# First feed-forward of a macaron layer: batches 4 to 7 go through a list of rows sorted by expert, in 15 tiles of 512 rows, instead of through all eight experts

## The chip, the core and the metric

The kernel runs on one core of a Trainium2 chip, in float32. The metric is the device time of one execution in microseconds (us). TensorE (PE) multiplies, VectorE (DVE), ScalarE (ACT) and GpSimd (POOL) work on its results, SyncE (SP) issues most of the DMAs. Each engine runs its own list of instructions strictly in the order in which they are written, and waits for the others by semaphores.

## The reference, cut to what matters

x is (8, 512, 128): 8 batches of 512 tokens. The layer is x + 0.5 FFN(norm(x)), then attention with 16 heads, then x + 0.5 FFN(norm(x)) again. The feed-forward:

```
probs = softmax(einsum('bsd,de->bse', x, gate_w) + gate_b, axis=1)     # over the tokens of a batch
vals, idx = top_k(probs, 2)                                            # 2 of 8 experts for each token
h = relu(einsum('bsd,edo->ebso', x, w1) + b1)                          # w1, w2, w3: (8, 128, 128)
h = relu(einsum('ebso,eop->ebsp', h, w2) + b2)
y = relu(einsum('ebso,eop->ebsp', h, w3) + b3)
w_tok = einsum('bske,bsk->bse', one_hot(idx), vals)                    # 0 for the experts not chosen
v = einsum('ebso,bse->eo', y, w_tok)                                   # one row for each expert, over all tokens
out = einsum('bse,eo->bso', one_hot(idx).max(axis=2), v)
```

A token's y for an expert counts only by its weight in v, and that weight is 0 for six of the eight experts. v sums over all tokens of all batches, so nothing behind it starts before the last of them is done.

## The kernel before, in words

**Units.** A feed-forward f (0 or 1) is 32 units (NU, line 43): unit u takes batches 2p and 2p+1 (p = u // 8), 1024 tokens as two halves of 512 columns, through expert e = u % 8. Each float32 product is three TensorE passes (high weights x high data, low x high, high x low), so a unit is 3 layers x 3 passes x 2 halves = 18 matmuls of 512 columns (`product` L739, `layer2` L758). DVE does the first activation in two instructions of 1024 columns (`split1_high` L1475, `split1_low` L1481). ACT does the second in two halves, relu and rounding (`relu2`, L1144 to L1167); POOL subtracts to get the low part (`split2`, L682). DVE does the third together with the weighting by w_tok and the sum over tokens in one instruction with an accumulator (`reduce3`, L1564 to L1577). The weights for that, spread to all 128 partitions, are in PU; one DMA of 512 KB for each unit, issued by SP, brings them from the DRAM tensor wd (`load_wb`, L509).

**Order.** `unit_steps` (L410) is one list that all engines walk: in iteration u stand layer 1 of unit u+2, its split, layer 2 of unit u+1, layer 3 of unit u, and then extra steps of a table (`GATE1` for the first feed-forward, L396). The PSUM pairs are a ring of four (`ring_table`, L234): each use waits until the use four earlier was drained.

**The gate of batches 4 to 7** is spread over iterations 0 to 12 by GATE1: normalize (ACT), transpose (PE), copy twice (ACT), low part (POOL), logits (PE), softmax, four steps of top-2 (`choose_late`, L1627), and the weights. The gate of batches 0 to 3 and the splitting of the weights are in `head` (DVE's from L1521), ahead of the units. Behind the units `update(0)` (L1685) turns the sums into the rows added to x; attention starts on them.

## Time and profile before

| | us |
|---|---|
| median of 3 runs | 1057.64 |
| lowest and highest of them | 1049.88, 1057.66 |
| profiled execution: span from the first to the last instruction | 1048.3 |
| device time given for the profiled execution itself | none; the lowest run is 1.6 above its span |
| busy share of the span: PE, DVE, ACT, POOL | 97%, 73%, 60%, 67% |
| granted TensorE clock, mean | 0.997 of full |

The first feed-forward's units run from about 18 to 176 us of the span, attention to about 900 us, the second feed-forward to the end. Shares of busy time are means over these stages. PE is called busy while a matmul is in flight, so 97% does not say that it could do no more; a stretch in which its matmuls start at a fixed distance does.

### The profile page before, as it was taken

Reading aid. Unit: us, or ns where it says so; the run is one execution under the profiler, and the core shown is the slowest. Engines: PE = TensorE matmul, PEld = TensorE weight load, DVE = VectorE, ACT = ScalarE, POOL = GpSimd, SP = SyncE. Lnnn points to the kernel's source line nnn. Section 1 sums busy time; section 2 is a strip of 40 time slices with the busy share of each in tenths; the row PEclk is TensorE's granted clock in tenths of the full one; section 3 lists DMA queues with packets and bytes.
Section 4 is the critical chain, followed back from the end, with each engine's and each line's share of the span. In section 5 each row is a group of like instructions: output and inputs, shape, how many; then the busy total and the mean of one; then the engine's idle time right before and its main releaser. Section 6 shows DMA issues by size and latency. Waiting matters only on the chain.

```text
span 1048.3 us, 18768 instructions
## 1 busy us (share of the span) xinstructions
PE 1015.9 (97%) x7176; PEld 661.9 (63%) x7176; DVE 763.9 (73%) x1027; ACT 632.1 (60%) x900; POOL 700.0 (67%) x369
## 2 busy tenths in 40 slices
PE   7999998899999999999999999999999999998996
PEld 6676886545657566556655665745565565776884
DVE  6879998877875676567576587546757636779996
ACT  4785556756754565456475477467746456775553
POOL 5555655766886588488488578756849757565653
PEclk9999999999999999999999999999999999999999
DMA  5721520000100100001001010001000103521612
GB/s 169 237 86 58 183 84 21 1 2 23 42 23 22 42 24 22 22 23 43 22 23 43 3 42 23 22 25 40 22 23 23 42 25 102 182 81 49 209 67 81
DMA packets 30253, 59.62 MB, mean 57 GB/s; under 512 B 10437, under 2 KB 15702, under 8 KB 30166
## 3 DMA queue, kind: packets, MB, share of 16 engines
q1 hardware_dynamic: 30096, 58.41, 18.4%
q8 instruction: 58, 0.95, 0.4%
q14 instruction: 29, 0.24, 0.1%
q10 hardware_dynamic: 70, 0.02, 0.0%
HBM read 55.27 MB, written 2.62 MB: 55 GB/s over the span
## 4 chain that ended last, share of the span: by engine, by line
PE 83%; DVE 10%; ACT 2%; issue 2%; POOL 2%; DMA 0%; DVEq 0%; ACTq 0%; POOLq 0%
PE ring L1038 20%; PE ring L972 6%; PE ring L1050 6%; PE ring L996 5%; PE ring L1002 5%; PE ring L998 5%; PE ring L1000 5%; PE ring L742 4%; PE ring L748 4%; PE ring L744 4%; PE ring L1011 3%; PE ring L766 2%; PE ring L765 2%; PE ring L768 2%; DVE ring L1576 2%
## 5 line engine op out<-in xcount | busy, mean ns | idle before, releaser
L1728 DVE TENSOR_REDUCE mx<-ring 128x2 f32<-128x1024 f32 x248 | 290.3, 1226 | 64.1 <-PE ring L972 64.1
L627 POOL TENSOR_TENSOR sum_picksT<-sum_picksT,P_wb 128x1024 f32<-128x1024 f32 x128 | 310.7, 2427 | 18.9 <-POOL sum_picksT L627 0.9
L1356 ACT ACTIVATE P_wb<-ring 128x1024 f32<-128x1024 f32 x256 | 262.1, 1026 | 54.2 <-PE ring L1002 24.6
L627 POOL TENSOR_TENSOR sum_picksT<-P_wb 128x1024 f32<-128x1024 f32 x64 | 167.0, 2610 | 167.8 <-ACT P_wb L1356 167.8
L686 POOL TENSOR_TENSOR R<-t,R 128x512 fp32r<-128x512 f32 x124 | 162.1, 1308 | 124.5 <-ACT R L1166 121.2
L1038 PE MATMUL ring<-P_wb,t 128*32 128x512 f32 x2048 | 228.4, 593 | 0.0
L1038 PEld LDWEIGHTS ring<-P_wb,t 128*32 128x32 f32 x2048 | 74.0, 110 | 138.6 <-issue 120.0
L1368 ACT COPY OZ<-ring 128x512 f32<-128x512 f32 x64 | 37.4, 585 | 157.3 <-PE ring L1038 148.6
L1166 ACT CAST R<-t 128x512 fp32r<-128x512 f32 x124 | 76.9, 620 | 74.6 <-PE ring L748 68.2
L972 PE MATMUL ring<-R 64*128 64x512 f32 x512 | 104.8, 407 | 1.0 <-ACT P_wb L1344 0.7
L996 PE MATMUL ring<-R 64*128 64x512 f32 x512 | 102.0, 393 | 1.5 <-DVE MR L1733 1.5
L1000 PE MATMUL ring<-R 64*128 64x512 f32 x512 | 101.1, 390 | 0.0
L998 PE MATMUL ring<-R 64*128 64x512 f32 x512 | 101.0, 390 | 0.0
L1002 PE MATMUL ring<-MR,NEG 64*128 64x512 f32 x496 | 98.3, 392 | 0.0
L1162 ACT ACTIVATE t<-ring,bcol 128x512 f32<-128x512 f32 x124 | 84.8, 684 | 20.8 <-PE ring L768 20.3
L1576 DVE SCALAR_TENSOR_TENSOR ring<-ring,nb,P_wb 128x1024 f32<-128x1024 f32 x62 | 80.0, 1290 | 13.3 <-PE ring L748 13.2
L742 PE MATMUL ring<-R,whi 128*128 128x512 f32 x252 | 81.5, 404 | 6.1 <-DVE MR L1485 1.8
L748 PE MATMUL ring<-R,whi 128*128 128x512 f32 x252 | 79.6, 396 | 0.0
L744 PE MATMUL ring<-R,wlo 128*128 128x512 f32 x252 | 79.6, 396 | 0.0
L972 PEld LDWEIGHTS ring<-R 64*128 64x128 f32 x512 | 48.2, 184 | 36.9 <-issue 24.9
L1753 DVE TENSOR_TENSOR OT_xnT<-OZ,rzb 128x1024 f32<-128x1024 f32 x32 | 70.0, 2188 | 0.0
L996 PEld LDWEIGHTS ring<-R 64*128 64x128 f32 x512 | 47.9, 184 | 34.6 <-ACT P_wb L1356 29.7
(199 smaller groups left out, 1529.9 us busy)
## 6 DMA issues: line engine op xcount, KB each, us to landing
P_wb<-wd SPq DMA_DIRECT2D x64, 512.0 KB, 4.8
rzb<-rzd SPq DMA_DIRECT2D x64, 256.0 KB, 3.9
xs<-in_L_attn_x SPq DMA_DIRECT2D x8, 256.0 KB, 5.2
zrc<-SZ SPq DMA_DIRECT2D x128, 2.0 KB, 1.7
out<-xs SPq DMA_DIRECT2D x8, 256.0 KB, 2.7
sum_picksT<-in_L_ffn_w SPq DMA_DIRECT2D x2, 512.0 KB, 5.6
MR<-mT SPq DMA_DIRECT2D x62, 4.0 KB
t<-in_L_ffn_w SPq DMA_DIRECT2D x1, 512.0 KB, 7.3
```

The source lines that it names most:

```text
L627: pool.tensor_tensor(US[:, g % 2, c, :, :], first, PU[:, TPB * c + t, :, :], ALU.add).then_inc(s_ua, 1)
L686: pool.tensor_tensor(low[:, k, :], t2[:, k, :], high[:, k, :].bitcast(F32), ALU.subtract).then_inc(s["h2_ready"], 1)
L742: pe.matmul(pair[:, k, :], whi[:, layer, e, :], high[:, k, :], start=True, stop=False)
L744: pe.matmul(pair[:, k, :], wlo[:, layer, e, :], high[:, k, :], start=False, stop=False)
L972: mm = pe.matmul(banks[:, par, :], QH[g % len(QH)][rows, c, P * j:P * (j + 1)], KH[rows, g // QUADS % 2, :], start=True, stop=True)
L996: pe.matmul(banks[:, par, :], KH[rows, kv, keys], QH[g % len(QH)][rows, c, :], start=True, stop=False)
L998: pe.matmul(banks[:, par, :], KH[rows, kv, keys], QL[g % len(QL)][rows, c, :], start=False, stop=False)
L1000: pe.matmul(banks[:, par, :], KL[rows, kv, keys], QH[g % len(QH)][rows, c, :], start=False, stop=False)
L1002: mm = pe.matmul(banks[:, par, :], less[rows, :], MR[rows, g % 2, c, :], start=False, stop=True)
L1038: mm = pe.matmul(weigh_bank(g, c)[row:row + SLOT, :], Vn[:, g // QUADS % 2, t, d:d + SLOT], PU[:, TPB * c + t, par, :], start=(t == 0), st ...
L1356: act.activation(PU[:, u, :, :], ring[slot(("scores", g, u))][:, :, :], ACT.Exp, scale=SCALE).then_inc(s_exp, 1)
L1728: dve.tensor_reduce(mx[:, :, u] if g else mx0_unit[:, u // TPB, :, 0, u % TPB, 0], ring[slot(("max", g, u))][:, :, :], AX.X, ALU.max).then ...
```

## The change

Only the first feed-forward changes in what it runs; units 0 to 15 (batches 0 to 3) stay. For batches 4 to 7 the 2048 tokens x 2 choices = 4096 rows are put into a DRAM list `rows_by_expert`, sorted by expert; each expert's part begins at a multiple of 512 rows (a tile). A row is 128 normalized values and 8 weights, 544 bytes. 15 tiles (8 + 7 for parts that are not full) run always; rows that nobody fills are zeros, written by 5 DMAs at the start. So units 16 to 31 become 8 units of two tiles (the last of one), 7.5 in place of 16.

- **Head:** POOL clears 1632 columns of `MR`, SP writes them five times to the list (4.2 MB). `MR` is also the buffer of unit 1's first activation: DVE waits for the five writes before `split1(0, 1)`.
- **Iterations 1 to 8:** normalized values go to `rows`; the copies to xh and xl for batches 4 to 7 go away; logits of four batches are taken at once; the four steps of top-2 stand in iterations 6 and 7 instead of 8 to 12. In 8, `count_rows` and `place_rows` work out each row's place and `tile_tables` each tile's expert and biases.
- **Iterations 8 to 12:** POOL sends the rows: 32 indirect DMAs of 128 rows, 7 in each iteration (4 in the last), behind its split2. In these iterations the second half of split2 is DVE's.
- **End of 12:** POOL copies the 768 columns of weights of tiles 0 to 7 to a buffer indexed by tile, two more tiles in each of iterations 16 to 19.
- **From 13 on:** each iteration begins with a `gather` for unit u+3: SP has loaded the rows, PE turns them (4 transposes for each tile), ACT rounds, DVE gets the row weights and the low part. SP writes the weights of a unit's rows out and spreads them back to PU.

```diff
+        RT = GROUPS * TPB * TPB * P // TS + E - 1
+        UNITS_OF = (DENSE + RU, NU)
+        def low_by_dve(f, u, k):
+            if f:
+                return k == 1 and u >= NU - 2
+            return u == UNITS_OF[0] - 1 or (k == 1 and SCATTERS.start <= u < SCATTERS.stop)
+        SCATTERS = range(8, 13)
-                 1: [("invert", 2), ("normal", 4)],
-                 2: [("turn", 4), ("normal", 5)],
-                 3: [("turn", 5), ("logits", 4), ("normal", 6)],
-                 4: [("turn", 6), ("logits", 5), ("normal", 7)],
-                 5: [("turn", 7), ("logits", 6)],
-                 6: [("logits", 7), ("largest", 1), ("exp", 1)],
-                 7: [("invert_sum", 1), ("probs", 1)],
-                 8: [("turn_probs", 1), ("choose", 0)],
-                 9: [("choose", 1)],
-                 10: [("choose", 2)],
-                 11: [("choose", 3)],
-                 12: [("picks", 1)]}
+                 1: [("invert", 2), ("normal", 4), ("normal", 5)],
+                 2: [("turns", 4), ("normal", 6), ("normal", 7)],
+                 3: [("turns", 6)],
+                 4: [("logits4", 4)],
+                 5: [("invert_sum", 1), ("probs", 1)],
+                 6: [("turn_probs", 1), ("choose", 0), ("choose", 1)],
+                 7: [("choose", 2), ("choose", 3)],
+                 8: [("counts", 1), ("ranks", 1)]}
+        for u in range(SCATTERS.start, SCATTERS.stop):
+            n = u - SCATTERS.start
+            GATE1.setdefault(u, []).extend(("scatter", k) for k in range(7 * n, min(7 * n + 7, 2 * TPB * TPB)))
+        GATE1[SCATTERS.stop - 1] += [("copy", r) for r in range(4)]
+        for r in range(4, RU):
+            GATE1.setdefault(DENSE + r - 4, []).append(("copy", r))
...
+            for u in range(last):
+                if u + 3 < last and routed(f, u + 3):
+                    steps.append(("gather", u + 3))
...
+            for part in range(5):
+                sp.dma_start(xg.rearrange("(p q r) c -> q p (r c)", p=P, q=5)[part], zeros).then_inc(s_zf, 16)
...
+                sp.wait_ge(s_sent, 16 * 2 * TPB * TPB)
+                routed_weights()
...
+            def scatter(n):
+                if n == 0:
+                    pool.wait_ge(s_places, 3)
+                    pool.wait_ge(s_zf, 16 * 5)
+                t = n % (TPB * TPB)
+                pool.indirect_dma_start(out=xg[:, :], out_offset=bass.IndirectOffsetOnAxis(ap=row_of[:, n:n + 1], axis=0),
+                                        in_=rows[:, t, :], in_offset=None).then_inc(s_sent, 16)
+            def copy_weights(r):
...
+                for k in halves_of(0, DENSE + r):
+                    e = pool.value_load(expert_int[0:1, 2 * r + k:2 * r + k + 1], min_val=0, max_val=E - 1)
+                    ins = pool.tensor_copy(WT[:, r % 4, k, :, :, :].rearrange("p l h o -> p (l h o)"),
+                                           wex[:, bass.ds(e, 1), :, :, :].rearrange("p e l h o -> p (e l h o)"))
...
+            def sorted_low(u):
+                r, n = u - DENSE, len(halves_of(0, u))
+                k = r % 2
+                dve.wait_ge(s_sorted[k], 16 * (r // 2 + 1))
+                wait(dve, s_rwd, 16 * (r - 1))
+                tiles = of_expert[:, 2 * r:2 * r + n, :].unsqueeze(2).to_broadcast([P, n, BLOCKS, E])
+                choice_link(dve.tensor_tensor(row_products[k][:, 0:n, :, :], sorted_rows[k][:, 0:n, :, P:ROW], tiles, ALU.mult))
+                dve.tensor_reduce(row_weights[k][:, 0:n, :], row_products[k][:, 0:n, :, :], AX.X, ALU.add).then_inc(s_rw, 1)
+                high, low = x_of(0, u)
+                dve.wait_ge(s_rxh, r + 1)
+                dve.tensor_tensor(low[:, 0:n, :], unit_pair(0, "gather", u)[:, 0:n, :], high[:, 0:n, :].bitcast(F32), ALU.subtract
+                                  ).then_inc(s_rxl, 1)
```

In a unit of tiles the two halves belong to two experts, so `split1_high`, `split1_low` and `reduce3` are two instructions of 512 columns each in place of one of 1024.

## Rows read from the trace of the kernel before

**Rows 1.** Busy time by stretch: engine, us (instructions), granted clock, DMA share, GB/s

```profile
30.00:40.00 10.00, 10.00 (x42) 8.06 (x42) 9.93 (x34) 6.76 (x11) 5.42 (x5) 0.96 1.02 271
49.00:58.00 9.00, 8.74 (x36) 5.59 (x37) 5.19 (x6) 8.50 (x17) 5.90 (x5) 1.00 0.20 69
100.00:170.00 70.00, 70.00 (x303) 56.30 (x302) 65.06 (x67) 41.74 (x67) 41.49 (x33) 1.00 0.37 121
```

**Rows 2.** Order of time, DVE, a unit beside the gate: start us, us, what

```profile
93.88 0.55 DVE L1625 TENSOR_TENSOR OZ<-OZ,tm 128x128 f32<-128x128 f32 x1
...
95.01 1.26 DVE L1479 TENSOR_SCALAR R<-ring,nb 128x1024 fp32r<-128x1024 f32 x1
96.31 1.28 DVE L1485 SCALAR_TENSOR_TENSOR R<-ring,nb,R 128x1024 fp32r<-128x1024 f32 x1
97.51 1.28 DVE L1576 SCALAR_TENSOR_TENSOR ring<-ring,nb,P_wb 128x1024 f32<-128x1024 f32 x1
...
98.71 0.42 DVE L1679 TENSOR_REDUCE wsum<-ring 128x8 f32<-128x256 f32 x1
```

**Rows 3.** Order of time, DVE, first units, seventh unit, and the units' end

```profile
27.08 1.27 DVE L1479 TENSOR_SCALAR MR<-ring,nb 128x1024 fp32r<-128x1024 f32 x1
...
67.19 1.29 DVE L1576 SCALAR_TENSOR_TENSOR ring<-ring,nb,P_wb 128x1024 f32<-128x1024 f32 x1 [0.25 <-PE ring L748]
...
174.20 0.69 DVE L1495 TENSOR_TENSOR R<-t,R 128x512 fp32r<-128x512 f32 x1
174.81 0.75 DVE L1571 SCALAR_TENSOR_TENSOR ring<-ring,nb,P_wb 128x512 f32<-128x512 f32 x1
...
175.48 0.76 DVE L1571 SCALAR_TENSOR_TENSOR ring<-ring,nb,P_wb 128x512 f32<-128x512 f32 x1
```

**Rows 4.** Order of time, DVE, small instructions in a chain

```profile
16.22 0.23 DVE L1545 TENSOR_SCALAR ring<-ring,gbc 128x1 f32<-128x1 f32 x1
16.48 0.22 DVE L1546 TENSOR_SCALAR gst<-ring,gbc 128x1 f32<-128x1 f32 x1
...
20.41 0.29 DVE L1616 TENSOR_REDUCE tm<-ring 128x16 f32<-128x128 f32 x1 [2.27 <-PE ring L854]
20.74 0.30 DVE L1617 TENSOR_TENSOR ring<-ring,tm 128x128 f32<-128x128 f32 x1
```

**Rows 5.** POOL's groups by form: xcount, busy us, mean ns, idle before

```profile
L686 POOL TENSOR_TENSOR R<-t,R 128x512 fp32r<-128x512 f32 x124 | 162.1, 1308 | 124.5 <-ACT R L1166 121.2 <-ACT R L1157 3.0
L655 POOL TENSOR_TENSOR wlo<-sum_picksT,whi 128x1024 fp32r<-128x1024 f32 x2 | 4.7, 2382 | 0.0
L612 POOL MEMSET ident<- 128x128 f32 x1 | 0.2, 204 | 0.3 <-POOLq L1878 0.3
```

**Rows 6.** SP's queue in order of time: start us, us that issuing took, what

```profile
10.44 0.43 SPq L489 DMA_DIRECT2D wos<-in_L_attn_Wq  x1
...
25.44 0.33 SPq L518 DMA_DIRECT2D wd<-sum_picksT  x1
26.99 4.46 SPq L511 DMA_DIRECT2D P_wb<-wd  x8
```

**Rows 7.** DMA issues to 60 us: KB each, median us to landing

```profile
P_wb<-wd SPq DMA_DIRECT2D x13, 512.0 KB, 6.3
wd<-sum_picksT SPq DMA_DIRECT2D x1, 64.0 KB, 1.5
```

**Rows 8.** PE and ACT groups: transposes, from 40 to 80 us; ACT's rounding in order of time

```profile
L854 PE MATMUL ring<-ident,xn 128*128 128x128 f32 x16 | 2.5, 276 | 1.1 <-ACT xn L1261 1.0
...
16.15 1.07 ACT L1170 CAST whi<-sum_picksT 128x1024 fp32r<-128x1024 f32 x1
```

**Rows 9.** Busy time by stretch, as rows 1, around a pause of PE

```profile
24.00:26.00 2.00, 0.43 (x2) 0.25 (x2) 1.90 (x5) 0.27 (x1) 1.16 (x1) 1.00 0.00 0
...
28.00:30.00 2.00, 2.00 (x6) 1.54 (x5) 1.96 (x5) 1.94 (x4) 0.62 (x1) 0.50 0.91 346
...
31.00:32.00 1.00, 1.00 (x6) 0.83 (x5) 1.00 (x7) 0.00 (x0) 0.91 (x1) 1.00 1.06 340
```

More of the change, by code:

```diff
@@ L7 @@
 F32R = mybir.dt.float32r
+I32 = mybir.dt.int32
 ALU = mybir.AluOpType
@@ L156, in macaron_kernel @@
         MR = sb("MR", [P, 2, PAIRS, S], F32R)
+        ZROWS = RT * TS // P // 5
+        zeros = MR[:, :, :, :].rearrange("p g c s -> p (g c s)")[:, 0:ZROWS * ROW].bitcast(F32)
         xh = R[:, 0:E, :]
@@ new lines, in gather, with turn_rows @@
+            def gather(u):
+                r = u - DENSE
+                k = r % 2
+                pe.wait_ge(s_sorted[k], 16 * (r // 2 + 1))
+                wait_unit(pe, 0, "gather", u)
+                for half in halves_of(0, u):
+                    mm = turn(unit_pair(0, "gather", u)[:, half, :], lambda j: sorted_rows[k][:, half, j, 0:P])
+                mm.then_inc(s_rx, 1)
+            def turn_rows(b, bank):
+                pe.wait_ge(F[0]["xn_done"], b + 1)
+                turn(bank, lambda j: rows[:, TPB * (b - TPB) + j, 0:P]).then_inc(F[0]["xn_transposed"], 1)
@@ L889, in units @@
                         layer3(f, arg)
+                    elif stage == "gather":
+                        gather(arg)
                     elif stage in UNIT_USES:
@@ L894, in units @@
                             sums(arg, bank)
+                        elif stage == "turns":
+                            turn_rows(arg, bank)
+                            turn_rows(arg + 1, other)
+                        elif stage == "logits4":
+                            for b in range(TPB, B):
+                                logits(f, b, bank)
+                        elif stage == "counts":
+                            pe.wait_ge(s["wtk_ready"], 2)
+                            turn_indicators(bank[:, 0:2 * P]).then_inc(s["picks_transposed"], 1)
+                            pe.matmul(other[:, 0:NT * E], ones[:, :], wtk[:, :, :, :].rearrange("p g e t -> p (g e t)"),
+                                      start=True, stop=True).then_inc(s["picks_transposed"], 1)
+                            pe.wait_ge(s["wtk_ready"], 3)
+                            pe.wait_ge(s_const, 5)
+                            pe.matmul(other[:, NT * E:NT * E + E], ones[:, :], chosen_by_p, start=True, stop=True)
+                            pe.matmul(other[:, NT * E + E:NT * E + 2 * E], before, chosen_by_p, start=True, stop=True).then_inc(s["picks_transposed"], 1)
+                        elif stage == "ranks":
+                            pe.wait_ge(s_ind_taken, f + 1)
+                            pe.wait_ge(s_mask, 1)
+                            pe.matmul(bank[:, 0:P], indT[:, 1, :], before_same, start=True, stop=True).then_inc(s["picks_transposed"], 1)
                         elif stage == "turn":
@@ L1256, in attention_normal, with normal_rows, sorted_high @@
                 normal(b, s_axn, 0)
+            def normal_rows(b):
+                for j in range(TPB):
+                    t = TPB * b + j
+                    ins = act.activation(rows[:, t - TPB * TPB, 0:P], xs[:, t, :], ACT.Identity, bias=nmr[:, t:t + 1], scale=rstd[:, t:t + 1])
+                ins.then_inc(F[0]["xn_done"], 1)
+            def sorted_high(u):
+                r = u - DENSE
+                n = len(halves_of(0, u))
+                act.wait_ge(s_rx, r + 1)
+                wait(act, F[0]["l1_done"], u - 1 if r >= 2 else 0)
+                act.copy(x_of(0, u)[0][:, 0:n, :], unit_pair(0, "gather", u)[:, 0:n, :]).then_inc(s_rxh, 1)
             def normal(b, done, home=None):
@@ L1293, in units @@
                 s = F[f]
-                moments_of = {2: 5, 3: 5, 7: 7} if f else {b: 1 for b in range(TPB, B)}
+                moments_of = {2: 5, 3: 5, 7: 7}
                 for stage, arg in unit_steps(f):
@@ L1454, in _ @@
                 dve.memset(prio[:, e:e + 1], float(E - e))
+            for i in range(2 * E):
+                dve.memset(count_up[:, i:i + 1], float(i))
+            for buffer in running:
+                dve.memset(buffer[:, 0:TPB], 0.0)
             ln_count = [0]
```

466 lines of the change are left out of this document (345 added, 121 removed).

## The prediction

> **What bounds the kernel now.** I read the busy time by stretch first, then DVE's order of time, then POOL's groups and SP's queue. The change touches only the first feed-forward, so only the first 176 us matter. In [rows 1] the steady stretch, 100 to 170 us, has PE busy for all 70 us: 16.7 units, 4.2 us each, 18 matmuls that start 0.233 us apart. What the row also says is that DVE is busy 65 of the 70. In [rows 2] a unit's three instructions of 1024 columns start 1.30, 1.20 and 1.20 us apart, 3.7 us of DVE. So PE sets the pace with 0.5 us to spare on DVE: whoever removes PE work has to remove DVE work too. Beside the gate of batches 4 to 7 the pace is 4.2 plus whatever PE and ACT have to add ([rows 1], 49 to 58: PE 8.7 of 9, ACT 8.5 of 9).
>
> **What a unit of tiles costs.** PE: 4.2 plus 8 transposes. 16 of them took 2.5 us [rows 8], so +1.2: 5.4. ACT: two relus and roundings, about 2.6, and a rounding of 1024 columns, 1.07 [rows 8]: 3.7. DVE: halves of 512 columns start 0.67 apart (174.81 and 175.48 in [rows 3]), so split and reduce3 are 6 x 0.67 = 4.0, with the waits between them 4.1; sorted_low is two small instructions (0.2 to 0.3 each by [rows 4]) and one of 1024 columns (1.2): 1.7. Together 5.8. DVE becomes the bound of these units, and 7.5 x 5.8 = 43.5 replaces 16 x 4.2 = 67.2. That is 23.7 us off, before everything that has to be paid for it.
>
> **The sum, along the path, in the times of the profiled execution.**
>
> 1. *Zeros.* 4.2 MB go through the queue on which the inputs landed until about 16 us. At the 346 GB/s of [rows 9] or the 271 of [rows 1] this is 12 to 16 us, so the buffer comes free at 28 to 32; DVE wanted it at 27.08 [rows 3]. PE is waiting for this split, nothing covers it. +3 (0 to +6; the weights' DMA queues behind the zeros but is needed later by as much).
> 2. *Iterations 0 to 6.* ACT and POOL lose the copies to xh and xl and the rows of logits, about 5 us on ACT. PE keeps all its work and was nearly full, so -1 (-3 to 0). reduce3(6), at 67.19 before [rows 3], starts at 69.2.
> 3. *From there to the row numbers,* all on DVE: 14 chained instructions of the top-2 at 0.33 apart [rows 4], with stretched ones as the 0.55 in [rows 2], 5.8 together; two more for rows and counts, 0.7; two splits 5.0; three reduce3 3.6; waiting for the matmuls 0.5; sums 0.42 [rows 2]; seven links of 8 columns at 0.26 [rows 4], 1.8; the places, 1.9. The row numbers are ready at 69.2 + 19.7 = 89. The same steps before lay in five iterations under PE's 4.2; now they are packed in three.
> 4. *Sending the rows.* 32 indirect DMAs, s us each in POOL's queue, and four split2 halves of 1.3 [rows 5] between them: T = 89 + 32 s + 5.2. PE cannot go ahead: layer 3 of the next unit waits for the low part that stands behind the 7 sends in POOL's queue. No row shows such a DMA. Below, s is 0.3 to 0.43, the time in which SP's queue issues a plain one [rows 6]; above, 1.3, POOL's instruction on 512 columns, or at worst 2.4, its 1024 columns [rows 5]. POOL has to walk 128 partitions and make 128 rows' addresses in software, which is nearer to its own instructions than to SP's issue: I take 1.1. Then T = 129.4. DVE needs only 4.4 us for such an iteration, so it waits.
> 5. *The first tiles.* SP waits for the last send to land (1.5 us for a small write, [rows 7]) and loads 557 KB (5, from the 6.3 of [rows 7] for 512 KB in a crowded stretch): PE's first gather starts at T + 6.5 = 136. It stands at the head of iteration 13, so PE stands still. Meanwhile POOL copies 8 tiles' weights. 768 columns lie between 0.7 (the 0.20 of 128 cleared columns [rows 5], scaled) and 1.8 (its two-input rate); with reading the expert 0.9 to 2.0, I take 1.2: 9.6, done at T + 9.6, about when split2(14) is asked for, so nothing; at 2.0 each it costs 5.
> 6. *From the first gather to the end,* DVE-bound: turning and rounding before DVE's first part, 2.3; sorted_low 13; split(15) 2.5; splits of tiles 20; reduce3 3.6 + 10.3; the rest 1.2; drain of the last unit 4: together 57. End at 193. SP's round trip for the row weights (1.5 + 6.3, [rows 7]) fits in the three units it has, about 17.
>
> The last reduce3 ended at 176.2 [rows 3]. 193 - 176.2 = **+17 us**, and behind it nothing changes: the update's extra instruction is 0.3, attention and the second feed-forward run the same instructions from other addresses.
>
> The end is 157.6 + 32 s (rounded), so the change breaks even at s = 0.58. Below s = 0.44 POOL no longer sets the pace; then DVE's own list of about 72 us behind the row numbers does, which with the drain ends at 165 to 171.
>
> The Trainium skill speaks against the change here ("DMA: Bandwidth & Descriptors", section on latency and other measured facts): a DMA made by GpSimd's software has its first byte after about 1 us, and it lays that on the emission of descriptors. Taking that as s, an estimate from that page, the end is 189.6, +13. No row here shows it.
> For the copies the skill ("GPSIMD Engine Reference", engine selection) says that one-input work runs at roughly line rate. By it they would be near the lower price, and the sum stays as it is; nothing here shows it.
>
> **Rivals.**
>
> *A. Cheap sends: faster.* If POOL only hands over the list and s is near SP's 0.43 [rows 6], sending hides in the iterations of 4.4 us. Place: POOL's queue in iterations 8 to 12. It decides from s below 0.58. At 0.43 the formula gives 171.4, -5; DVE's own list gives -10 at best. For it: SP's row. Against: even then the gain is 10 of 1048, since the tiles cost DVE 5.8 each. Time 1048 to 1053.
>
> *B. Sends of 0.6 to 0.9,* or dearer ones with a head that costs nothing: +2 to +10. Time 1059 to 1067.
>
> *C. Sends at POOL's far price, or slowed by DVE:* s of 1.6 to 2 gives +33 to +45. For it: instructions that take two operands from SBUF on DVE and POOL at once were stretched (0.55 against 0.30, [rows 2, 4]). With it goes PE's clock: in [rows 9], after a pause at 24 to 26 with 0.43 busy of 2, the granted clock was 0.50, the 1.2 GHz level, from 28 to 30, and full again at 31. A pause of about 10 us before the first gather would bring that once, some 2 us; in the sending iterations PE has 4.2 of 9 us, and matmuls twice as long (0.47) may lengthen the chain layer 3, layer 2, relu, split2 there by 2 to 3 us an iteration, some 10. Time 1085 to 1103.
>
> *D. It doesn't skip what it says.* 15 tiles run whether full or not, 7680 rows for 4096; that is already in the sum. There is nothing that could make it 16.
>
> **How the numbers follow.** The profiled span is 1048.3 and its own device time isn't given, the lowest run is 1.6 above; the median is 0.7% higher than that. The three runs lie 0.7% apart, so 1% (10.6 us) is about what can be told from no change. I put +17 on the median: 1057.6 + 17 = 1074.6, for s between 0.9 and 1.5: chance 0.50. C 0.13, B 0.25, A 0.12. All of B, and A where it gains under 1%, are "same"; A reaches 1% only with everything hidden, but my list of DVE may be too long by some per cent of 72 us, or the units quicker than I think, so faster keeps 0.10; same 0.27, slower 0.63. Range: low end s = 0.45 to 0.5, about -6, 1051; high end s = 1.6 or s = 1.1 with the slow clock and dear copies, +43 less what these share, 1098.
>
> **What would show it.** In the profile after: the unit of tiles at 5.8 us with DVE near full; POOL's queue holding 32 DMAs that start s apart, and PE idle behind POOL's split2 from about 90 to 130; a pause of 6 to 10 us on every engine but POOL before the first gather; the last reduce3 at about 193; split(0, 1) 3 us late. Wrong if the sends start under 0.6 apart, or if the last reduce3 is before 176.

## The result, and where the 33 us are

The changed kernel took 1083.13 us (median of 4 runs, 1082.82 to 1084.19) against 1054.91 us (median of 4) for the kernel before: the ratio is 1.0282, with a 95% interval of 1.0242 to 1.0321. It is slower by some 28 us where the forecast said 17. The profiled execution took 1082.82 us with a span of 1081.0; that is 32.7 more than the span of before (1048.3), and these two traces are what is compared below. The two spans lie further apart than the medians because the profiled execution of the kernel before is the fastest of its four (1049.88 us; the slowest took 1057.66).

The page of the changed kernel first: its chain of waits by engine and by line, as shares of the span.

```profile
PE 76%; DVE 12%; POOL 5%; issue 3%; ACT 2%; DMA 1%; POOLq 0%; DVEq 0%; ACTq 0%
PE ring L1232 20%; PE ring L1166 6%; PE ring L1244 5%; PE ring L1190 5%; PE ring L1196 5%; PE ring L1192 5%; PE ring L1194 5%; PE ring L903 3%; PE ring L909 3%; PE ring L1205 3%; PE ring L905 3%; POOL rows_by_expert L831 3%; PE ring L1147 1%; POOL sum_picksT L761 1%; PE ring L930 1%
```

The line to see is `POOL rows_by_expert L831 3%`: 3% of 1081 us, some 32 us, of the work that ended last is POOL issuing sends. It is the only new line of that size. Everything behind the first feed-forward is merely shifted: a step of DVE near the attention's end starts at 899.34 us before and at 932.40 now, the attention's first maximum at 202.88 and at 235.99: 33.1 us both times. So all of the loss is made ahead of 236 us.

**The row numbers.** DVE in order of time: start, us, what. The row numbers are cast to integers at 87.87 us; POOL had been waiting for just that, as the release in brackets says.

```profile
87.87 0.18 DVE L1956 CAST xn<-xn 128x32 int32<-128x32 f32 x1
...
88.34 1.15 POOL L831 DMA_INDIRECT rows_by_expert<-sum_picksT,xn  x1 [3.53 <-DVE xn L1956]
89.79 0.96 POOL L831 DMA_INDIRECT rows_by_expert<-sum_picksT,xn  x1 [0.30 <-issue]
```

The last two are POOL's first sends. From the second on, most of them take 0.96 us with 0.30 us of idle time ahead of each that has no releaser, so they start 1.26 us apart. The group over the stretch from 88 to 136 us, and the end of the queue:

```profile
L831 POOL DMA_INDIRECT rows_by_expert<-sum_picksT,xn x32 | 31.8, 992 | 12.4 <-issue 8.9 <-DVE xn L1956 3.5
```

```profile
127.98 2.49 POOL L823 TENSOR_TENSOR R<-t,R 128x512 fp32r<-128x512 f32 x2
...
134.45 0.96 POOL L831 DMA_INDIRECT rows_by_expert<-sum_picksT,xn  x1 [0.30 <-issue]
135.41 0.83 POOL L841 CAST tile_weights<-wex 128x768 fp32r x1
```

32 sends keep POOL busy for 31.8 us and idle for 8.9 us of "issue" between them, and five low halves of layer 2 stand among them (6.3 us). Two of these stand at 127.98, ahead of the last four sends. The last send ends at 135.41.

**The wait.** SP holds the load of the sorted rows behind the last send. The rows of SP and DVE:

```profile
136.75 0.89 SPq L635 DMA_DIRECT2D sum_picksT<-rows_by_expert  x2
...
140.38 1.33 DVE L1738 TENSOR_TENSOR xn<-sum_picksT,OZ 128x64 f32<-128x64 f32 x1 [18.41 <-DMA sum_picksT<-rows_by_expert]
```

DVE was idle for 18.41 us up to 140.38. The busy time by stretch (columns as in [rows 1]) shows it for all engines:

```profile
110.00:120.00 10.00, 6.65 (x19) 4.81 (x17) 4.51 (x5) 2.49 (x4) 8.05 (x8) 0.67 0.14 49
120.00:130.00 10.00, 0.51 (x2) 0.00 (x0) 1.35 (x2) 1.84 (x4) 8.15 (x9) 0.50 0.14 49
130.00:140.00 10.00, 0.00 (x0) 0.00 (x0) 0.00 (x0) 0.00 (x0) 8.91 (x11) 0.50 0.29 90
```

From 120 to 140 us PE is busy for 0.51 us of 20, and in the last ten only POOL works at all. Before, PE had no gap from 100 to 170 us [rows 1]. From 100 to 120 us PE and DVE are already down to about half of their time (11.0 and 8.6 of 20 us busy), since the low half that PE needs is queued behind seven sends: PE waits 5.62 us for it at 108.83 and 3.35 us at 119.29. The granted clock is at 0.50, the lower of its two levels (1.2 GHz), from 120 to 144 us. It had been there before, from 108 to 112 us, behind the 5.62 us in which PE waited.

**The units of tiles.** The costliest DVE groups from 140 to 207 us (count | busy us, mean ns | idle before), and one unit in order of time:

```profile
L1823 DVE SCALAR_TENSOR_TENSOR ring<-ring,xn,P_wb 128x512 f32<-128x512 f32 x15 | 16.5, 1141 | 2.4 <-PE ring L909 2.4
...
L1738 DVE TENSOR_TENSOR xn<-sum_picksT,OZ 128x64 f32<-128x64 f32 x7 | 4.5, 640 | 18.4 <-DMA sum_picksT<-rows_by_expert 18.4
```

```profile
171.48 1.40 DVE L1703 TENSOR_SCALAR MR<-ring,xn 128x512 fp32r<-128x512 f32 x2
...
174.24 1.16 DVE L1823 SCALAR_TENSOR_TENSOR ring<-ring,xn,P_wb 128x512 f32<-128x512 f32 x1
175.28 1.18 DVE L1823 SCALAR_TENSOR_TENSOR ring<-ring,xn,P_wb 128x512 f32<-128x512 f32 x1
...
177.90 1.40 DVE L1703 TENSOR_SCALAR R<-ring,xn 128x512 fp32r<-128x512 f32 x2
```

The next unit begins 6.42 us after this one, and DVE has next to no idle time in it (19.72 of 20 us busy from 160 to 180). A half of the reduction (L1823) starts 1.04 to 1.06 us after the one before it; in the kernel before the two last ones were 0.67 apart [rows 3]. The small product of sorted_low (L1738) takes 0.21 to 0.28 us where it is undisturbed and 0.64 in the mean. Where it is long, POOL is at work:

```profile
160.21 2.59 POOL L823 TENSOR_TENSOR R<-t,R 128x512 fp32r<-128x512 f32 x2 [3.84 <-ACT R L1349]
...
161.71 1.17 DVE L1738 TENSOR_TENSOR xn<-sum_picksT,OZ 128x64 f32<-128x64 f32 x1
```

POOL's two products end at 162.80 and DVE's 64 columns, begun at 161.71, at 162.88.

**The end.** DVE's last reductions, and what POOL did beside them:

```profile
201.77 2.34 POOL L788 TENSOR_TENSOR wqlo<-wos,wqhi 128x1024 fp32r<-128x1024 f32 x1 [2.23 <-ACT wqhi L1354]
...
202.30 2.36 DVE L1729 TENSOR_TENSOR R<-t,R 128x512 fp32r<-128x512 f32 x1
...
205.62 1.14 DVE L1823 SCALAR_TENSOR_TENSOR ring<-ring,xn,P_wb 128x512 f32<-128x512 f32 x1 [0.96 <-PE ring L909]
```

The low product of 128x512 takes 2.36 us here and took 0.69 us in the kernel before [rows 3]; POOL's 2.34 us product for the attention starts 0.53 us ahead of it, and the two end 0.55 us apart. The last reduction ends at 206.76 where it ended at 176.24 before. Behind it, PE and the clock:

```profile
208.00:212.00 4.00, 3.21 (x13) 1.30 (x13) 1.38 (x2) 0.66 (x2) 0.00 (x0) 0.50 0.00 0
```

The clock is at 0.50 when the update starts, and the first maximum of the attention comes 29.2 us behind the last reduction instead of 26.6.

### The profile page after: what moved, and what is told of

It reads as the page before. It is cut to its first block, busy times and chain, and to the rows that moved or that the text cites. A ratio compares the mean times of both kernels' runs of the same rounds, so it can differ in the third digit from the quotient of the medians.

```text
span 1081.0 us, 18697 instructions
## 1 busy us (share of the span) xinstructions
PE 1003.7 (93%) x7088; PEld 650.6 (60%) x7088; DVE 764.9 (71%) x1099; ACT 613.0 (57%) x865; POOL 712.7 (66%) x394
## 4 chain that ended last, share of the span: by engine, by line
PE 76%; DVE 12%; POOL 5%; issue 3%; ACT 2%; DMA 1%; POOLq 0%; DVEq 0%; ACTq 0%
PE ring L1232 20%; PE ring L1166 6%; PE ring L1244 5%; PE ring L1190 5%; PE ring L1196 5%; PE ring L1192 5%; PE ring L1194 5%; PE ring L903 3%; PE ring L909 3%; PE ring L1205 3%; PE ring L905 3%; POOL rows_by_expert L831 3%; PE ring L1147 1%; POOL sum_picksT L761 1%; PE ring L930 1%
## 5 line engine op out<-in xcount | busy, mean ns | idle before, releaser
L823 POOL TENSOR_TENSOR R<-t,R 128x512 fp32r<-128x512 f32 x103 | 134.6, 1309 | 126.7 <-ACT R L1349 126.3
L1349 ACT CAST R<-t 128x512 fp32r<-128x512 f32 x111 | 68.8, 620 | 70.6 <-PE ring L909 65.2
L1344 ACT ACTIVATE t<-ring,bcol 128x512 f32<-128x512 f32 x96 | 65.6, 684 | 39.8 <-PE ring L933 22.0
L909 PE MATMUL ring<-R,wex 128*128 128x512 f32 x190 | 64.4, 418 | 15.2 <-POOL R L823 9.5
L1842 DVE SCALAR_TENSOR_TENSOR ring<-ring,nb,P_wb 128x1024 f32<-128x1024 f32 x47 | 60.6, 1290 | 21.6 <-PE ring L909 21.6
L903 PE MATMUL ring<-R,wex 128*128 128x512 f32 x190 | 63.8, 418 | 3.1 <-DVE MR L1717 1.8
L905 PE MATMUL ring<-R,wex 128*128 128x512 f32 x190 | 61.8, 407 | 0.0
```

The lines of the kernel that those rows point to most:

```text
L823: pool.tensor_tensor(low[:, k, :], t2[:, k, :], high[:, k, :].bitcast(F32), ALU.subtract).then_inc(s[f"h2_low{k}"], 1)
L903: pe.matmul(pair[:, k, :], weights_of(f, u, k, layer, 0), high[:, k, :], start=True, stop=False)
L909: mm = pe.matmul(pair[:, k, :], weights_of(f, u, k, layer, 0), low[:, k, :], start=False, stop=True)
```

## Experiments

Twelve kernels were run, each a variant of the changed kernel. Their spans are compared with its 1081.0 us; where a kernel was timed in rounds, the ratio to the kernel before is given. Seven of them (1, 3 to 7 and 11) were executed once. The four executions of the changed kernel lie within 1.4 us of each other in span and those of experiment 10 within 4.6, so of a single execution a few us of span prove nothing by themselves; there the rows of the trace carry the argument.

### 1. The weights read without a stride

```diff
-mm = turn(unit_pair(0, "gather", u)[:, half, :], lambda j: sorted_rows[k][:, half, j, 0:P])
+columns = unit_pair(0, "gather", u)[:, half, :].rearrange("p (t j) -> p j t", j=BLOCKS)
+for j in range(BLOCKS):
+    mm = pe.transpose(columns[:, j, :], sorted_rows[k][:, half, j, 0:P], ident[:, :])
 ...
-z = expert_pair(0, 3, u)[:, k, :].rearrange("p (j t) -> p j t", j=BLOCKS)
+z = expert_pair(0, 3, u)[:, k, :]
-    in1=PU[:, r, k, :].rearrange("p (t j) -> p j t", j=BLOCKS),
+    in1=PU[:, r, k, :],
```

> The whole computation stays; the four transposes of a tile write every fourth PSUM column, so that the tile's columns stand in the order of the row weights, and the reduction of a half reads the weights one after the other instead of 16 bytes apart. Theory: it is this reading that makes a half of the reduction start 1.06 us after the other instead of the 0.67 of the kernel before. Then the halves are 0.67 apart, the unit of tiles falls from 6.4 to about 5.6 us and the span by 15 x 0.39 = 5.9 us, to about 1075. Rival: the extra time comes from the tile's bias operand or from GpSimd's weight copies beside it; then the halves stay at 1.06 and the span stays at 1081.

1076.11 us, span 1074.3, so 6.7 less. The group of the reductions over the same stretch, and in order of time DVE's and POOL's products at the end:

```profile
L1825 DVE SCALAR_TENSOR_TENSOR ring<-ring,xn,P_wb 128x512 f32<-128x512 f32 x15 | 10.7, 752 | 3.5 <-PE ring L909 3.5
```

```profile
199.58 0.68 DVE L1731 TENSOR_TENSOR R<-t,R 128x512 fp32r<-128x512 f32 x1
...
199.81 2.68 POOL L788 TENSOR_TENSOR wqlo<-wos,wqhi 128x1024 fp32r<-128x1024 f32 x1 [2.23 <-ACT wqhi L1356]
```

15 halves take 10.7 instead of 16.5 us, 0.75 each instead of 1.14. Nothing but the order in which the operand is read was changed (with the columns permuted at the transposes to match), so 5.8 us are the stride, and the rival falls. The units start 5.6 to 6.5 us apart, not always 5.6 as the theory had it. From the landing of the rows to the end of the last reduction it is 61.2 instead of 66.4 us. The rest of the account: the small products waited 0.7 us more for POOL (5.2 against 4.5), the tail 1.1 more for PE (3.5 against 2.4), and the last low part took 0.68 instead of 2.36, because it happened to start 0.23 us ahead of POOL's product instead of behind it; now POOL's is the longer one, 2.68 us. The clock stayed at 1.00 into the update, and with it the first maximum of the attention came 27.1 us behind the last reduction instead of 29.2; that gives the rest of the gain.

### 2. Eight sends instead of 32

```diff
-GATE1.setdefault(u, []).extend(("scatter", k) for k in range(7 * n, min(7 * n + 7, 2 * TPB * TPB)))
+GATE1.setdefault(u, []).extend(("scatter", k) for k in range(7 * n, min(7 * n + 7, 8)))
 ...
-sp.wait_ge(s_sent, 16 * 2 * TPB * TPB)
+sp.wait_ge(s_sent, 16 * 8)
```

> Leaves out 24 of the 32 indirect DMAs (rows of 3 of 4 token groups are not sent; all 15 tiles still run). Theory: GpSimd's queue sets the pace of iterations 8 to 12, so up to 24 x 1.26 = 30 us go, less where DVE takes over as the bound (about 4.4 to 5 us an iteration): span 1050 to 1055, no gain over the kernel before even with three quarters of the sends for nothing. Rival: the sends are hidden and the time is lost in the loading of sorted rows and in the tiles; then the span falls by less than 10.

1050.46 us (median of 10 runs), ratio to the kernel before 0.9986 (0.9968 to 1.0004); span 1047.3, so 33.7 less than with all of them. The rows of 24 sends never reach the list here, so this kernel does not compute the layer; it prices the sends. Without those 24 the whole loss is gone. DVE around the change from the dense units to the tiles, and at the end:

```profile
105.23 1.29 DVE L1842 SCALAR_TENSOR_TENSOR ring<-ring,nb,P_wb 128x1024 f32<-128x1024 f32 x1 [0.66 <-PE ring L909]
110.43 1.29 DVE L1842 SCALAR_TENSOR_TENSOR ring<-ring,nb,P_wb 128x1024 f32<-128x1024 f32 x1 [0.67 <-PE ring L909]
...
111.64 0.81 DVE L1738 TENSOR_TENSOR xn<-sum_picksT,OZ 128x64 f32<-128x64 f32 x1
...
173.99 1.12 DVE L1823 SCALAR_TENSOR_TENSOR ring<-ring,xn,P_wb 128x512 f32<-128x512 f32 x1 [0.91 <-PE ring L909]
```

The rows are there when DVE comes to them (no wait at 111.64) and the dense units are 5.20 us apart. Still the last reduction ends at 175.1, only 1.1 us ahead of the kernel before: with three quarters of the sends gone there is nothing to gain. From the first rows to the end DVE needs 63.5 us, for three dense units and for tiles at 6.4 us a unit, and before them the work on the row numbers and five dense units at 5.2 instead of 4.2 us had used up the rest of the saving.

### 3. Sends of 64 rows

```diff
-out_offset=bass.IndirectOffsetOnAxis(ap=row_of[:, n:n + 1], axis=0),
-in_=rows[:, t, :], in_offset=None
+out_offset=bass.IndirectOffsetOnAxis(ap=row_of[0:64, n:n + 1], axis=0),
+in_=rows[0:64, t, :], in_offset=None
```

> Each of the 32 indirect DMAs sends 64 rows instead of 128 (leaves out half of the rows). Theory of a price by the row (GpSimd writes an address for each row): a send falls from 1.26 to about 0.8 us, the span by about 15 to 1066. Rival, a fixed price of the instruction: sends stay 1.2 to 1.26 apart and the span at 1080.

1079.57 us, span 1077.8. POOL's group and two of its sends:

```profile
L831 POOL DMA_INDIRECT rows_by_expert<-sum_picksT,xn x31 | 28.7, 926 | 8.9 <-issue 8.9
```

```profile
89.36 0.89 POOL L831 DMA_INDIRECT rows_by_expert<-sum_picksT,xn  x1 [0.30 <-issue]
90.56 0.89 POOL L831 DMA_INDIRECT rows_by_expert<-sum_picksT,xn  x1 [0.30 <-issue]
```

With half of the rows a send takes 0.89 instead of 0.96 us, and the 0.30 us ahead of it are the same: they start 1.20 us apart. So 64 rows are worth 0.06 us and, if the rest scales in the same way, 1.14 are paid per instruction. The last send ends 3.65 us earlier than in the changed kernel, but 1.6 of that was there before the first send (86.73 against 88.34 us), so 2.0 are the smaller sends. The theory of a price by the row fell.

### 4. The low halves of the dense units on DVE

```diff
-return u == UNITS_OF[0] - 1 or (k == 1 and SCATTERS.start <= u < SCATTERS.stop)
+return u == UNITS_OF[0] - 1 or (k == 1 and u == 8) or 9 <= u <= 13
```

> The whole computation stays; in units 9 to 13 DVE subtracts both halves of the second activation's low part, so GpSimd has nothing but the sends from 88 to 129 us. If GpSimd's queue is the path: five instructions of 1.3 us leave it, the last send ends 6.5 us earlier and the span falls by 6.5 to about 1074.5; DVE's five instructions of 0.7 more are in its pauses and cost nothing. Rival: layer 3's wait behind the sends is what holds everything up, not the end of the sends; then PE runs free through iterations 8 to 12 and the gain is more than 10.

1076.54 us, span 1074.1, so 6.9 less. POOL's last send and DVE's wait:

```profile
113.86 1.29 DVE L1842 SCALAR_TENSOR_TENSOR ring<-ring,nb,P_wb 128x1024 f32<-128x1024 f32 x1 [0.67 <-PE ring L909]
...
128.87 0.96 POOL L831 DMA_INDIRECT rows_by_expert<-sum_picksT,xn  x1 [0.30 <-issue]
...
134.94 1.18 DVE L1738 TENSOR_TENSOR xn<-sum_picksT,OZ 128x64 f32<-128x64 f32 x1 [19.73 <-DMA sum_picksT<-rows_by_expert]
```

The last send ends 5.6 us earlier and the rows land 5.4 us earlier. DVE has now done its dense reductions by 115.2 and waits 19.73 us instead of 18.41. PE's waits of 5.62 and 3.35 us for POOL are gone (it waits 0.96 to 0.98 us for DVE's low halves), the last of these reductions starts 6.8 us earlier, and none of it came back, since the end of POOL's queue is what all wait for. The last reduction of the feed-forward ends 4.5 us earlier; the rest of the 6.9 is the clock, which is back at 1.00 when the update's matmuls run (204 to 208 us). It was never PE's or DVE's time ahead of the wait that counted.

### 5. PE kept busy ahead of the rows

```diff
-pe.wait_ge(s_sorted[k], 16 * (r // 2 + 1))
 wait_unit(pe, 0, "gather", u)
+if r == 0:
+    warm(unit_pair(0, "gather", u)[:, 0, :], 130)
+pe.wait_ge(s_sorted[k], 16 * (r // 2 + 1))
```

> 130 transposes whose result nothing reads stand on PE ahead of the first gather from the sorted rows, in the pause in which PE waits for them. Theory 1 (the clock at half after that pause is a small part of the loss): PE shows the full clock from 140 us on, and the span falls by about 2 us, because DVE and not PE sets the pace of the units of tiles. Rival (DVE has slack once PE is fast): 5 us or more. Second rival: no change at all, since PE's slow stretch lies beside DVE's work anyway.

1081.65 us, span 1079.8. DVE at the head and at the first rows, and the window row of the start of the tiles:

```profile
27.59 1.28 DVE L1708 TENSOR_SCALAR MR<-ring,nb 128x1024 fp32r<-128x1024 f32 x1 [0.20 <-DMA rows_by_expert<-MR]
...
139.05 1.22 DVE L1740 TENSOR_TENSOR xn<-sum_picksT,OZ 128x64 f32<-128x64 f32 x1 [18.54 <-DMA sum_picksT<-rows_by_expert]
```

```profile
140.00:144.00 4.00, 4.00 (x20) 3.21 (x19) 3.21 (x5) 1.70 (x2) 0.18 (x1) 1.00 0.21 13
```

The clock is 1.00 where it was 0.50 (140 to 144 us). But the rows already landed 1.3 us earlier, because in this execution the clock happened to hold at the head too. From the landing to the last reduction the tiles took 66.0 us instead of 66.4. So the low clock at the start of the tiles cost 0.4 us, not 2: PE at half its clock lies beside DVE's work.

### 6. The last low part on POOL

```diff
-return u == UNITS_OF[0] - 1 or (k == 1 and SCATTERS.start <= u < SCATTERS.stop)
+return k == 1 and SCATTERS.start <= u < SCATTERS.stop
```

> In the last unit of tiles the low part of the weights is left to POOL instead of being computed on DVE. Theory (DVE's 2.36 us for it was an ordinary 0.69 us product slowed by POOL's neighbour at the same moment, and it stood on the path): the last reduction ends about 2 us earlier and the update finds the clock less far down, together 3 to 5 us of span. Rival (the end is set by POOL's own low part): no change or 1 us slower.

1077.93 us, span 1076.1, so 4.9 less. DVE's last reduction, and POOL's low part with the attention's product behind it:

```profile
200.03 1.29 POOL L823 TENSOR_TENSOR R<-t,R 128x512 fp32r<-128x512 f32 x1 [1.29 <-ACT R L1349]
...
201.27 2.38 POOL L788 TENSOR_TENSOR wqlo<-wos,wqhi 128x1024 fp32r<-128x1024 f32 x1
...
201.97 1.16 DVE L1823 SCALAR_TENSOR_TENSOR ring<-ring,xn,P_wb 128x512 f32<-128x512 f32 x1 [0.32 <-PE ring L909]
```

From landing to the end of the last reduction it is 63.3 instead of 66.4 us; on POOL the same low part costs 1.29 us and the product for the attention simply starts when it is done. The rest of the 4.9 is 0.5 of an earlier landing and an update that finds the clock at 0.72 (204 to 208 us) instead of 0.50. On DVE it had stood behind that product. The theory holds, and the rival (POOL's own low part as the new end) does not.

### 7. Fourteen warming transposes at the head

```diff
-warm(turned_bank(2), 8)
+warm(turned_bank(2), 14)
```

> The second run of warming transposes at the head of the kernel is 14 instead of 8 long. Theory (the 1.7 us that the first split lost came from PE's clock after a pause at 9 us, not from the zeros that are written to the list): the first split starts near 24.6 us again, the window 12 to 16 us shows a clock near 1.00, and the span falls by 1.7 us. Rival (the writes of the zeros, or the loads behind them, hold it up): the clock is back and the start of the splits is not.

1082.23 us, span 1080.4. DVE's first split in the changed kernel:

```profile
26.29 1.26 DVE L1706 TENSOR_SCALAR R<-ring,nb 128x1024 fp32r<-128x1024 f32 x1
```

and the first two here, with a window row:

```profile
24.54 1.26 DVE L1706 TENSOR_SCALAR R<-ring,nb 128x1024 fp32r<-128x1024 f32 x1
28.36 1.28 DVE L1706 TENSOR_SCALAR MR<-ring,nb 128x1024 fp32r<-128x1024 f32 x1 [1.24 <-DMA rows_by_expert<-MR]
```

```profile
12.00:16.00 4.00, 3.62 (x22) 1.79 (x22) 3.27 (x8) 3.81 (x8) 2.88 (x3) 1.00 0.89 262
```

With the clock at 1.00 (0.57 before this edit in the same window) the first split starts 1.75 us earlier, at 24.54. The second one then waits 1.24 us for a DMA that reads the tile MR: it is the buffer from which the zeros are written to the list. So both readings hold in part: the clock cost 1.7 us, and behind it the zeros hide a wait of up to 1.2 us of their own. The edit is not shown to be what held the clock. In the changed kernel it fell twice, to 0.57 from 12 to 16 us and to 0.50 from 20 to 22. In experiments 5 and 8 it stayed at 1.00 up to 24 us without this edit (first split at 24.80 and 24.46), and in experiments 10 and 12 it fell to 0.50 from 18 to 20 us with it (26.29 and 26.02). The span falls by 0.6, and the rows land 1.5 earlier.

### 8. The tiles' steps behind the dense units

```diff
+if f == 0 and DENSE - 3 <= u < DENSE:
+    held += [step for step in here if routed(f, step[1])]
+    here = [step for step in here if not routed(f, step[1])]
 ...
+if f == 0 and u == DENSE - 1:
+    steps += held
 ...
-return u == UNITS_OF[0] - 1 or (k == 1 and SCATTERS.start <= u < SCATTERS.stop)
+return 10 <= u < DENSE
 ...
+GATE1[8] += [("scatter", k) for k in range(2 * TPB * TPB)] + [("copy", r) for r in range(4)]
```

(with the weights read as in experiment 1)

> Weights read without the stride, all 32 sends in one go with no low part of a dense unit ahead of them on POOL (DVE computes those), and the tiles' steps moved behind the last dense units, so that no engine waits for the rows before its dense work is done. All of the computation stays. Theory (three separate losses that add: POOL's queue about 6, the stride about 7, dense work that stood behind the wait about 8): sends end near 129, rows land near 134, the last reduction of the feed-forward ends near 190, span 1062 to 1066; still slower than the kernel before, since POOL's 32 sends alone end later than the dense units do. Rival (moving the wait only moves the idle time): no better than 1070.

1080.68 us, ratio 1.0272 (1.0236 to 1.0308), span 1077.9: the theory missed by 12 us and more. The sends did end early, at 125.4, but the dense units stood still meanwhile. DVE in order of time:

```profile
105.11 1.29 DVE L1848 SCALAR_TENSOR_TENSOR ring<-ring,nb,P_wb 128x1024 f32<-128x1024 f32 x1 [5.48 <-remote]
...
116.35 1.28 DVE L1712 TENSOR_SCALAR R<-ring,nb 128x1024 fp32r<-128x1024 f32 x1 [9.89 <-issue]
...
129.90 1.29 DVE L1848 SCALAR_TENSOR_TENSOR ring<-ring,nb,P_wb 128x1024 f32<-128x1024 f32 x1 [9.74 <-remote]
```

Three gaps of 5.48, 9.89 and 9.74 us, and for none does the trace name a releaser that explains it: "remote" and "issue". At the end of the first and of the third, ACT resumes within 0.1 us of DVE (105.04 and 129.82 us), which points to something that both waited for. PE's records have the matmuls that DVE waits for done at 100.2 and 101.6, and PE itself is idle (0.39 us busy from 110 to 120). What held the units is not settled.

### 9. The same with eight sends

```diff
-GATE1[8] += [("scatter", k) for k in range(2 * TPB * TPB)] + [("copy", r) for r in range(4)]
+GATE1[8] += [("scatter", k) for k in range(8)] + [("copy", r) for r in range(4)]
 ...
-sp.wait_ge(s_sent, 16 * 2 * TPB * TPB)
+sp.wait_ge(s_sent, 16 * 8)
```

> The same kernel as e8_sends_behind_dense with 8 of its 32 sends; the 24 others are left out, so the rows of those tokens never reach the list. It bounds what the change could give if the sends were cheap. Theory (the price of the change is the number of sends on POOL's queue, and 15 tiles are worth something only when they can start before the dense units end): 24 sends of 1.26 us less, of which some 5 us lie beside dense work, so span 1036 to 1042, about 1 per cent faster than the kernel before. Rival (the tiles' own steps eat the gain, as in e2): within 0.5 per cent of before.

1058.2 us (median of 10), ratio to the kernel before 1.0061 (1.0041 to 1.0082), span 1059.2. By the medians that is 7.7 us more than the eight sends in their first places, by the two profiled spans 11.9 (this execution took 1061.49 us), and the forecast was wrong in its sign. The gaps of experiment 8 are gone, but the rows at DVE show what the moved steps cost:

```profile
136.45 0.23 DVE L1744 TENSOR_TENSOR xn<-sum_picksT,OZ 128x64 f32<-128x64 f32 x1 [2.58 <-DMA sum_picksT<-rows_by_expert]
...
184.22 0.76 DVE L1829 SCALAR_TENSOR_TENSOR ring<-ring,xn,P_wb 128x512 f32<-128x512 f32 x1 [1.08 <-PE ring L913]
```

With the first gather behind the last dense unit there is nothing between the two kinds of unit: DVE waits 2.58 us for rows and 2.60 for ACT's rounding, at a clock of 0.71 from 130 to 140 us, and the last reduction ends at 185.0 instead of 175.1, although the stride's 5.8 us are saved. Part of it is that DVE also has both low halves of six dense units here (one such pair took 3.69 us instead of 1.28 beside POOL's copies of weights); how much is that and how much the moved steps was not told apart. Moving them was my mistake, and it is one of two reasons why experiment 8 missed.

### 10. The small edits together

> The single edits that each took something off are put together: weights read without the stride (6.7 us alone), both low halves of the dense units 9 to 13 on DVE (6.9), the last low part on POOL (4.9), the longer warming at the head (0.6) and the transposes ahead of the first gather (1.2). The sends stay spread as in the changed kernel, and no step is moved. Theory (the losses are separate and add): their sum is 20 us, so a span near 1061 and 1 per cent slower than the kernel before, because the 32 sends alone hold the rows back until 134. Rival (they overlap, since a faster DVE only waits longer at PE or POOL): 1068 or more.

(Edits 1, 5, 6 and 7 with `return (k == 1 and u == 8) or 9 <= u <= 13` for 4.) 1075.82 us, ratio 1.0201 (1.0155 to 1.0247), span 1074.6, no better than edit 1 or 4 alone. Up to the end of the feed-forward the edits did add: rows at 133.17 (140.38), last reduction done at 196.0 (206.8). Then the first maximum of the attention came at 229.34, later than in experiment 1 (228.80), where the last reduction had ended at 201.7. The windows show where it went:

```profile
190.00:194.00 4.00, 2.60 (x8) 1.34 (x8) 1.62 (x5) 2.72 (x4) 2.69 (x3) 1.00 0.00 0
198.00:202.00 4.00, 3.22 (x13) 1.22 (x13) 1.49 (x3) 0.79 (x2) 0.13 (x1) 0.50 0.47 130
```

PE is busy for 2.6 of 4 us from 190 to 194 and its clock falls to 0.50 behind it; the update's 16 matmuls take 5.1 us instead of 3.2, and the clock is at 0.50 up to 206 us and at 0.69 again from 218 to 229. The rival (they overlap) gave the number, by another mechanism than it named.

### 11. The moved steps without the rest

> As e10_all_small without the transposes ahead of the gather, and with the tiles' steps held behind the last dense unit, as in e8_sends_behind_dense; unlike there the units 14 and 15 have their low parts on POOL and the sends stay spread. It asks what stopped PE for 25 us between 100 and 130 in e8_sends_behind_dense. Theory 1 (that stop belongs to the moved steps): it shows here too, span 1070 or more. Theory 2 (it belongs to the sends in one go or to the low parts of units 14 and 15 on DVE): no stop, the dense work of units 14 and 15 lies ahead of the wait for the rows, and the span is 5 to 8 us under that of e10_all_small.

1079.19 us, span 1077.3. The diff is that of 10, less edit 5, with the `held` lines of 8. PE and POOL:

```profile
127.91 6.21 POOL L848 CAST tile_weights<-wex 128x768 fp32r x8
...
135.40 0.80 PE L916 MATMUL ring<-R,wex 128*128 128x512 f32 x1 [14.67 <-POOL R L830]
```

No unnamed gap: the dense units run 5.8 us apart up to 117.6. So the moved steps alone are not what stopped PE in experiment 8, and of theory 2 that much holds. The rest of it failed on something visible: unit 14's low half was on POOL behind all sends and eight copies of weights, and PE waited 14.67 us for it. Of the two causes that theory 2 names, the low halves of 14 and 15 on DVE are in experiment 9 as well, which has no gap. So it takes all 32 sends in one go, alone or with something else, and by what means was not found.

### 12. PE kept busy at the end

```diff
+if f == 0 and u >= UNITS_OF[0] - 2:
+    warm(expert_pair(f, 3, u)[:, 0, :], 11)
 ...
-warm(expert_pair(f, 2, UNITS_OF[f] - 1)[:, 0, :], 14 if f else 10)
+warm(expert_pair(f, 2, UNITS_OF[f] - 1)[:, 0, :], 14 if f else 24)
```

> As e10_all_small, with transposes whose result nothing reads in the waits of PE at the end of the tiles: 11 ahead of layer 3 of each of the last two units and 24 instead of 10 ahead of the update. In e10_all_small the feed-forward ended 5.8 us earlier than in e1_plain_weights, but PE's granted clock fell to 0.50 at 195 us and the first maximum of the attention came at the same time (229.3 and 228.8). Theory (the clock took the 5 us back): the clock stays at 1.00 from 186 to 210 us, the 16 matmuls of the update take 3.2 instead of 5.1 us, the first maximum comes near 224 and the span is 1068 to 1070, still 1.5 per cent slower than the kernel before. Rival (the fall has another cause than PE's pauses, or something else of the attention's start holds): 1073 or more.

1071.88 us, ratio 1.0178 (1.0135 to 1.0221), span 1072.2. The same windows as in 10:

```profile
190.00:194.00 4.00, 3.90 (x26) 2.98 (x24) 1.62 (x5) 2.65 (x5) 2.71 (x3) 1.00 0.00 0
198.00:202.00 4.00, 3.21 (x17) 1.18 (x17) 2.42 (x9) 0.79 (x2) 1.09 (x1) 1.00 0.46 135
```

The clock holds and the update takes 3.21 us again; the first maximum comes at 226.09, 3.2 us earlier. The forecast was 224 and 1068 to 1070. The clock fell after all, somewhat later, to 0.73 from 214 to 218 us and 0.89 up to 240. This is the best of the variants with all of the computation, and it is 1.8% slower than the kernel before. No run points to a version that beats the kernel before. Fewer and longer sends, with more than 128 rows in each, were not tried.

## Why the prediction was right in sign and short in size

The forecast was +17 us to 1074.6, slower at 0.63, in a range of 1051 to 1098. It was laid on the median of three runs (1057.64); with the fourth the median before is 1054.91. The path that it named is the one that the traces show; what was short is the size of some terms. By its steps:

1. **Zeros, +3 at the head.** None of it showed in the changed kernel. The writes and loads ran at 422 GB/s from 16 to 24 us and were through by 26. What came instead was a clock of 0.57 from 12 to 16 us and of 0.68 from 20 to 24 (1.00 before), worth +1.7: in the four experiments in which it held up to 24 us (5, 7, 8, 11) the first split starts at 24.46 to 24.80 us, in the four in which it fell only behind 16 us (3, 6, 10, 12) at 25.96 to 26.29. The zeros' own wait was 0.2 and 1.2 us in experiments 5 and 7. A kernel without zeros was not tried.
2. **Iterations 0 to 6, and the row numbers.** The seventh reduction started at 67.96 (forecast 69.2) and the numbers were there at 88.05 (forecast 89): right to 1.2 us, though partly by luck, as the 1.7 of the clock stands where 3 were laid on the zeros.
3. **The sends.** The mechanism was right: the end of POOL's queue is the path (experiments 2 and 4), and SP, DVE and PE stand behind it. The size of s was not: 1.26 us where 1.1 was taken, which is 32 x 0.16 = 5.1 us, and five low halves stood among them instead of four (1.3). The break-even of s = 0.58 was too generous: even with a quarter of the sends, as much as s = 0.32 for all of them, the change only ties. The Trainium skill ("DMA: Bandwidth & Descriptors", latency and other measured facts) has about 1 us to the first byte of such a DMA, and the prediction's estimate from it was +13. No trace here shows the first byte; POOL is busy for 0.96 us with each, and the next one only starts 0.30 later.
4. **The landing.** 4.97 us from the end of the last send to the rows at DVE, where 6.5 were taken (-1.5). First rows at 140.38 against 136.
5. **The copies of weights at no cost.** Right: 0.78 us apart instead of 1.2, in POOL's time behind the last send. That one-input work runs at roughly line rate on POOL is what the Trainium skill says ("GPSIMD Engine Reference", engine selection).
6. **The units of tiles, 57 us from the first gather to the end.** This term failed most: 66.4. The unit of two tiles took 6.42 us instead of 5.8. Three durations had been taken from rows in which the operand was contiguous and POOL stood still. The stride made a half of the reduction 1.14 instead of 0.75 us, 5.8 in all (experiment 1). The seven small products took 4.5 us instead of 1.5, behind POOL. The last low part took 2.36 instead of 0.69, worth 3.1 with what hangs on it (experiment 6). These come to 11.9, more than the 9.4 that were missing, and they do not add: with the stride alone mended the tiles take 61.2 us (experiment 1), and in experiment 10, which moves the last low part too, 62.8. The low clock at the start was 0.4 (experiment 5). Rival C had read the stretched instructions in [rows 2] as a mark of DVE and POOL in each other's way; it should have stood in the sum.
7. **Not in the sum:** the clock at 0.50 when the update starts, which puts 2.6 us between the last reduction and the attention (29.2 instead of 26.6).

The sum: 4.4 (later rows) + 9.4 (tiles) + 2.6 (clock) = 16.4 on top of 17 is 33.4, against 33.1 at the attention's first maximum and 32.7 in the spans.

**The rivals.** A, cheap sends, was priced at -5 to -10 us; experiment 2 gives this case -1.0 with a quarter of them: the tiles' own price, too low in the forecast, takes the rest. B, s of 0.6 to 0.9, did not hold (1.26). C, s near its far end or the clock at half throughout, named the side on which the miss lay, with +33 to +45, and the span came out at its edge, though by the tiles and not by s. Its slow clock in the sending iterations did come (0.50 from 108 to 112 us), but POOL never waited for another engine between its first send and its last, so it cost nothing there. D, tiles that run whatever their rows, is how the kernel works (15 tiles always).

## What to carry to other kernels

An indirect DMA of 128 rows of 544 bytes was charged to POOL by the instruction: count such instructions before the bytes, and look at what stands behind them in the same queue that others need. When a stage is priced from rows of another, ask of every operand whether it will be read in the same order and who will be working beside it. Where an edit makes a stage shorter, look at the clock in the stage behind it before you credit the gain.

## What was not expected of the hardware

- **A send is priced mostly by the instruction.** 128 rows held POOL for 0.96 us and 64 rows for 0.89, each with 0.30 us ahead of it.
- **A stride is paid on DVE.** The reduction of 128x512 takes 0.75 us with its second operand contiguous in SBUF and 1.14 us when that is read with a stride of 16 bytes.
- **DVE and POOL take turns.** DVE's product of 64 columns, begun inside POOL's, ended 0.08 us behind it (1.17 us instead of 0.22); the one of 512 columns, begun 0.53 us behind POOL's, took 2.36 us; begun 0.23 us ahead of POOL's in experiment 1 it took its 0.68, and POOL's was the longer. The Trainium skill says this of the port pair that the two share ("SBUF — State Buffer", two separate sides), for a DVE instruction with two inputs in SBUF beside a GpSimd one that reads SBUF: whichever starts first holds the pair for its whole instruction. All three places, products of two SBUF operands, agree.
- **The clock can take a gain back.** PE at 2.6 busy of 4 us fell to a granted clock of 0.50 (1.2 GHz) right behind (experiment 10) and held 1.00 (2.4 GHz) with 3.9 of 4 (experiment 12). In experiment 1 it held at 1.00 with 2.60 of 4 us busy and 1.93 of 4 behind that, so the fall isn't certain and its cause is open.
- **Open:** DVE stood still for 25 us in three gaps of experiment 8 with no releaser in the trace; it did not with 8 of the 32 sends (experiment 9).
